# A routed two-layer network on one core: expert results are added into one row per token by indirect DMA, instead of being stored per choice and summed after a gather

## The reference

```
topv, topi = top_k(logits, K)            # K = 4, then 2
w   = softmax(topv)
sel = exp_out[token, topi]               # K rows of 128 per token
out = sum_k w[k] * sel[k]
x   = layernorm(x + out)
```

## Time and profile before

| | |
|---|---|
| median of 3 runs | 964.85 us (964.06 to 967.42) |
| span of the profiled execution, its own time | 1145.5 us |
| mean granted TensorE clock in it | 0.858 |
| PE / DVE / POOL / ACT busy | 73% / 57% / 46% / 45% |
| tiles of the first and second mixture | 76 and 36 (152 and 72 scatters of results) |

### The profile page before, as it was taken

The page is one execution under the profiler, slowest core; times in us unless marked ns, Lnnn a source line. Parts: engine busy times, 40 slices in busy tenths (PEclk is TensorE's granted clock), DMA queues, the critical chain, the costliest instruction groups (busy, mean ns, idle before and its releaser), DMA issues.

```text
span 1145.5 us, 35350 instructions
## 1 busy us (share of the span) xinstructions
PE 835.4 (73%) x11802; PEld 642.2 (56%) x11816; DVE 652.7 (57%) x1923; ACT 509.8 (45%) x1290; POOL 525.7 (46%) x538
## 2 busy tenths in 40 slices
PE   4898886877886513887788888847788839999920
PEld 1565555555565401766677667735555529888810
DVE  5457555455544520666565566647787636656656
ACT  2555444444433311544444445426454226656623
POOL 1013634546343471455554555541666644554433
PEclk9899888898857755999898999979887869999965
DMA  6011211112111123433333333323231124222243
GB/s 192 21 31 38 66 34 50 43 44 61 36 48 33 38 74 90 83 68 82 71 79 69 78 86 86 81 85 130 88 122 39 38 84 67 57 55 50 51 131 108
DMA packets 136238, 79.73 MB, mean 70 GB/s; under 512 B 104402, under 2 KB 116857, under 8 KB 136144
## 3 DMA queue, kind: packets, MB, share of 16 engines
q1 hardware_dynamic: 122256, 51.76, 18.7%
q0 software_dynamic: 13312, 25.31, 7.1%
q10 hardware_dynamic: 576, 1.34, 0.4%
HBM read 33.12 MB, written 32.63 MB: 57 GB/s over the span
## 4 chain that ended last, share of the span: by engine, by line
PE 48%; issue 13%; DVE 13%; another core or an unknown queue 9%; ACT 5%; SPq 4%; POOL 4%; DMA 2%; ACTq 1%; DVEq 0%; POOLq 0%
PE avbank L1736 6%; PE proj L1736 5%; PE avbank L1589 4%; PE t L1576 3%; PE t L1717 3%; PE s L1717 3%; PE s L1715 2%; PE t L1715 2%; PE s L1716 2%; PE t L1716 2%; ACT act_out L1359 2%; PE s L1539 2%; POOL xs L655 2%; PE t L1784 2%
## 5 line engine op out<-in xcount | busy, mean ns | idle before, releaser
L714 POOL DMA_INDIRECT yt<-ysb,to_now x224 | 236.8, 1057 | 260.7 <-ACT ysb L1346 197.4
L655 POOL DMA_INDIRECT xs<-x1p,sidx x192 | 189.8, 989 | 196.5 <-ACT prob L1265 111.7
L944 DVE CAST h_hi<-act_out 128x512 bf16<-128x512 f32 x152 | 73.6, 484 | 147.2 <-ACT act_out L1359 113.9
L945 DVE TENSOR_TENSOR h_lo<-act_out,h_hi 128x512 bf16<-128x512 f32 x152 | 107.9, 710 | 5.2
L1265 ACT ACTIVATE prob<-t 128x384 f32<-128x384 f32 (+1 forms) x160 | 74.4, 508 | 78.0 <-PE t L1576 66.1
L1715 PE MATMUL s<-xt,w_hi 128*128 128x256 bf16 x296 | 82.8, 280 | 17.8 <-DMA xt<-xs 13.3
L1736 PE MATMUL avbank<-w_hi,h_hi 128*128 x448 | 89.8, 230 | 7.6 <-issue 6.4
L1736 PE MATMUL avbank<-w_hi,h_lo 128*128 x448 | 87.7, 229 | 3.6 <-issue 3.3
L1736 PE MATMUL avbank<-w_lo,h_hi 128*128 x448 | 87.3, 228 | 2.4 <-issue 2.4
L1736 PE MATMUL proj<-w_hi,h_hi 128*128 x448 | 83.6, 220 | 7.2 <-DVE h_lo L945 5.6
L1717 PE MATMUL t<-xt,w_lo 128*128 128x256 bf16 x296 | 81.5, 275 | 5.9 <-issue 5.9
(11 more groups left out here) (235 smaller groups left out, 2131.4 us busy)
## 6 DMA issues: line engine op xcount, KB each, us to landing
w_raw<-w_all SPq DMA_DIRECT2D x59, 256.0 KB
gat<-yt SPq DMA_DIRECT2D x7, 1024.0 KB, 5.3
gat<-yt SPq DMA_DIRECT2D x10, 512.0 KB, 4.5
yt<-ysb,to_now POOLq DMA_INDIRECT x224
xs<-tail_rows SPq DMA_DIRECT2D x24, 129.0 KB
xs<-x1p,sidx POOLq DMA_INDIRECT x192
out<-ow SPq DMA_DIRECT2D x8, 256.0 KB, 2.3
xt<-xs SPq DMA_TRANSPOSE x112
```

The costliest lines, as they stand in the source:

```text
L655: pool.indirect_dma_start(out=xs[n][:, :], out_offset=bass.IndirectOffsetOnAxis(sidx[:, par, at:at + 1], 0), in_=x1p[:, par, t, k, :], in_ ...
L714: pool.indirect_dma_start(out=yt[n][:, :], out_offset=bass.IndirectOffsetOnAxis(to_now[:, u, s:s + 1], 0), in_=ysb[:, u, s, :], in_offset= ...
L944: ch.link(dve.tensor_copy(h_hi[:, par, c, :], act_out[:, par, c, :]))
L945: dve.tensor_tensor(h_lo[:, par, c, :], act_out[:, par, c, :], h_hi[:, par, c, :], ALU.subtract).then_inc(split_done[n], 1)
```

## The change

`yt` is gone. For each mixture there is `acc`, one row of 128 floats per token (and 256 rows for padding). It is filled with the residual (`fill_sums`, one 256 KB store per batch on SP, as soon as the batch's rows are kept). The weight of a choice travels with the row: two more bf16 places in `xs` hold it as a float, written by `weigh`. ACT multiplies by it when it takes a tile out of PSUM, with two activations of 128x128 in place of one copy of 128x256, and therefore waits for `to_loaded` now. The scatters add to `acc` instead of overwriting (`compute_op=ALU.add`), with no bounds check.

A tile's scatters wait until those of the preceding tile have landed; the two tiles may hold the same token for different choices. `scale_results`, `pair_up`, `add_up` and the weighted sums of `final_sums` are gone; a batch's load is 256 KB in place of 1024 KB or 512 KB, with 2 KB contiguous per partition (`acc[0]` and the output are laid out "(p t)"). The final scales are double buffered. `tile_table` gets one more column (`new_of`), which nothing reads; one more DVE operation, one more PE transpose and one more DVE conversion make it.

```
-                        pool.wait_ge(to_loaded[n][u], 16 * g + 16)
                         pool.wait_ge(y_done[n], RING * g + u + 1)
-                        pool.sem_inc(sending[n], 1)
+                        if u > 0 or not (type(g) is int and g == 0):
+                            pool.wait_ge(y_stored[n][u - 1 if u else RING - 1], 16 * S2 * (g + 1 if u else g))
+                        pool.sem_inc(sending, 1)
                         for s in range(S2):
                             pool.indirect_dma_start(
-                                out=yt[n][:, :], out_offset=bass.IndirectOffsetOnAxis(to_now[:, u, s:s + 1], 0),
-                                in_=ysb[:, u, s, :], in_offset=None, bounds_check=B * L * top[n] - 1,
-                                oob_is_err=False).then_inc(y_stored[n][u], 16)
+                                out=acc[n][:, :], out_offset=bass.IndirectOffsetOnAxis(to_now[:, u, s, 0:1], 0),
+                                in_=ysb[:, u, s, :], in_offset=None, compute_op=ALU.add).then_inc(y_stored[n][u], 16)
 
                 pool.wait_ge(table_kept[n], 1)
-                more = over_tiles(pool, n, group)
+                pool.wait_ge(acc_filled[n], 16 * B)
...
+            def fill_sums(n, b):
+
+                rows = acc[n][bass.ds(b * L, L), :]
+                rows = rows.rearrange("(p t) d -> p t d", p=P) if n == 0 else rows.rearrange("(t p) d -> p t d", p=P)
+                sp.wait_ge(x1_kept, B * n + b + 1)
+                apart(sp)
+                sp.dma_start(rows, xres[:, bass.ds(b * T, T), :]).then_inc(acc_filled[n], 16)
...
-                    act.wait_ge(yp_ready[n], j + 1)
                     if not (type(use) is int and use == 0):
                         act.wait_ge(y_stored[n][u], 16 * S2 * use)
-                    nc.scalar.copy(ysb[:, u, :, :], y_bank[u % 2][:, 0:S2 * D].rearrange("p (s d) -> p s d", s=S2)
-                                   ).then_inc(y_done[n], 1)
+                    act.wait_ge(to_loaded[n][u], 16 * use + 16)
+                    act.wait_ge(yp_ready[n], j + 1)
+                    for s in range(S2):
+                        ins = nc.scalar.activation(ysb[:, u, s, :], y_bank[u % 2][:, s * D:(s + 1) * D], ACT.Identity,
+                                                   scale=to_now[:, u, s, 1:2].bitcast(F32))
+                    ins.then_inc(y_done[n], 1)
...
                 if nxt:
-                    x2_apply(b + 1)
-                if nxt2:
-                    pair_up(b + 2, par)
-                    add_up(b + 2, par)
+                    x2_apply(b + 1, 1 - par)
                 take_logits(1, b)
...
                 if nxt2:
-                    y_stats()
+                    sum_stats(b + 2, par, i + 1)
```

More of the change, by code:

```diff
@@ L476, in _ @@
                     sp.dma_start(w_raw[:, k, :], w_all[:, bass.ds((2 * c + k) * CH, CH)]).then_inc(raw_in[k], 16)
+            def fill_sums(n, b):
[4 more added lines that the diff above has]
+                sp.dma_start(rows, xres[:, bass.ds(b * T, T), :]).then_inc(acc_filled[n], 16)
+            for c in range(1, CPB_0):
+                load_chunks(c)
+            with sp.Fori(2, B) as b:
+                for c in range(CPB_0 // 2):
+                    load_chunks(CPB_0 // 2 * b + c)
+                fill_sums(0, b - 2)
+            for b in range(B - 2, B):
+                fill_sums(0, b)
             def fill_tails(n):
@@ L554, in _ @@
             sp.wait_ge(all_stored[0], 1)
-            for half in range(2):
-                ts = slice(T // 2 * half, T // 2 * half + T // 2)
-                rows = slice(ts.start * P * K0, ts.stop * P * K0)
-                sp.dma_start(gat0[:, 0, ts, :, :], yt[0][rows, :].rearrange("(t p k) d -> p t k d", p=P, k=K0)
-                             ).then_inc(gathered[1][half], 16)
-            load_outputs(0, 1)
+            for b in range(2):
+                load_outputs(0, b)
             for b in range(B):
                 if b + 2 < B:
-                    sp.wait_ge(comb_done, b + 1)
+                    sp.wait_ge(x2_ready, b + 1)
                     load_outputs(0, b + 2)
+                if b:
+                    fill_sums(1, b - 1)
                 sp.wait_ge(lo_done, CHUNKS_0 + max(b - 1, 0))
@@ L1199, in _ @@
             dve.wait_ge(decay_ready, 1)
-            dve.wait_ge(x1_kept, B)
-            for half in range(2):
-                dve.wait_ge(gathered[1][half], 16)
-                for k in range(K0):
-                    for t in range(T // 2 * half, T // 2 * half + T // 2):
-                        ins = dve.scalar_tensor_tensor(out=y[:, t, :], in0=gat0[:, 0, t, k, :], scalar=wres[:, t, k:k + 1],
-                                                       in1=y[:, t, :] if k else xres[:, t, :], op0=ALU.mult, op1=ALU.add)
-                    if k < K0 - 1:
-                        ch.link(ins)
-            ins.then_inc(comb_done, 1)
-            dve.wait_ge(comb_done, 1)
-            y_stats()
-            x2_apply(0)
-            pair_up(1, 1)
-            add_up(1, 1)
-            y_stats()
+            sum_stats(0, 0, 0)
+            x2_apply(0, 0)
+            sum_stats(1, 1, 0)
             for e in range(T):
@@ L1702, in tile_table @@
                 pe.wait_ge(table_ready[n], 1)
[L1703 removed]
+                for c in range(3):
                     pe.transpose(xbank[0:1, c * P:(c + 1) * P], tile_e[:, 4 + c:5 + c], ident)
[L1706 removed]
+                ins = pe.matmul(xbank[0:1, 3 * P:3 * P + 1], tile_e[:, 3:4], fours[:, :], start=True, stop=True)
                 ins.then_inc(table_turned[n], 1)
```

178 lines of the change are left out of this document (76 added, 102 removed).

## The result

| | us |
|---|---|
| changed kernel, median of 4 runs | 1243.66 (1236.76 to 1246.38) |
| kernel before, beside it, median of 4 runs | 966.13 (964.06 to 967.76) |
| ratio | 1.2885, 95% interval 1.2833 to 1.2937 |
| predicted | 1045 (955 to 1150) |

The changed kernel is 29% slower. The direction was forecast, the size was not: the loss is 278 us where 80 were expected, and the time is outside the range.

The account below looks back on a forecast made before the run. It took PE and idle time to set the tiles now, and a serial scatter chain of 4.8 us per tile afterwards. Mixtures +60 and +19, savings and table -23: +56 on 1145.5, or 1012; with 1077 otherwise, the middle 1045 (955 to 1150).

Parts of the forecast that it names:

- The second way to the median: Both mixtures: tiles of 3.4 and 4.0 us grow to 4.8, adding 135 us, less 23 of savings: 1077 us.
- the recording stretches: Whole kernel: profiling lengthens the execution, so the 1145.5 us span stands for a median of 964.85, 0.842 of it.
- The middle between 1012 and 1077: Whole kernel: 1045 us, taken between shrinking everything alike (1012) and a chain that does not shrink (1077).
- a tile in series costs 1.28 + 2.41 = 3.69 us: Both mixtures: second scatter 1.28 us after the first, landing 2.41 us later, with plain scatters; 3.85 us mid-stage.
- an add does not repeat the issue on POOL: Result scatters of both mixtures: adding costs somewhat under half a round trip, 0.95 us per tile, larger descriptors included.
- The savings: Outside the tiles: stage (c)'s first load -5, six batches -4, final stage -15, larger table +1; 23 us saved.
- Cost 0 for ScalarE's take-out and its wait: Mixture tiles: two activations for one copy, +0.45 us per tile, hidden behind the chain; wait for `to_loaded` covered; cost 0.
- Rival 1: Mixtures: the wait is hidden, serial tile 3.7 to 3.85 us, only savings remain, about 942 us; chance 0.14.
- Rival 2: First mixture: PE's clock falls too, its tile lasts 5.5 us and PE is the bound, 1130 us; chance 0.10.
- Rival 3: Both mixtures: the add costs a whole trip, 6.26 us per tile, +276, 1240 us; chance 0.07.

Follow-up runs that it names:

- after_overwrite: Changed kernel with its scatters overwriting instead of adding, the wait for the preceding tile kept: 1094.15 us, ratio 1.1352.
- scatters_alone: No part of the kernel: 24 serial pairs of plain, then of adding scatters on an idle core, then again beside copies; alone 4.28 and 5.32 us per pair.
- before_serial: Kernel before with the new wait alone, each tile's plain scatters waiting for the preceding tile's to land: 1117.85 us, ratio 1.1589.
- weights_left_out: Changed kernel with ScalarE's old unweighted copy as take-out, not waiting for the tile's numbers (POOL waits for them): 1243.47 us beside 1243.66.
- hybrid_plain: Kernel before, own row per choice, no added waits; weight travels with the row, ScalarE applies it, final sums are wide additions: 969.32 us, ratio 1.006.

## Why the prediction was wrong

The chain was named rightly, and so was who waits for it; three terms were wrong, the tile before and the two parts of the tile in series. The second way to the median, by which a tile's growth is 1.4 and 0.8 us and the result 1077, makes the account. The growth was 5.99 - 2.92 = 3.07 us and 5.95 - 4.02 = 1.93. So 76 x 1.67 + 36 x 1.13 = 168 us are missing from it, and 1077 + 168 = 1245, which is the result to 1 us. The forecast of 1045 lacks 32 us more.

| per tile, us | forecast | measured, first / second mixture |
|---|---|---|
| tile before | 3.4 / 4.0 | 2.92 / 4.02 |
| plain tile in series | 3.85 | 4.70 / 4.54 (`after_overwrite`) |
| adding | 0.95 | 1.29 / 1.42 |
| tile after | 4.8 | 5.99 / 5.95 |

- **Step "the recording stretches" failed.** The second profile refutes it. It hid that the first mixture stood at 2.92 us per tile, with PE's own 2.76 and POOL's 2 x (1.07 + 0.30) = 2.73 just below. Half of the waiting of the earlier trace rows belonged to that one long execution: in the usual one 99.6 us of POOL's idle time end with `ysb`, not 197.4. This is 0.5 us per tile, 36 us. The middle between 1012 and 1077 went wrong for the same reason, by 32 us: there was nothing to shrink.
- **Step "a tile in series costs 1.28 + 2.41 = 3.69 us" failed.** The 2.41 us of the earlier trace rows end with a memset on POOL and a load on SP. A waiting plain scatter's record starts later: 3.00 us after the second one's start, with nothing else running (`scatters_alone`). The pair costs 4.28 us alone; in the kernel it costs 0.3 to 0.4 more, of which the weight load is 0.19 in the first mixture, and the prediction had allowed 0.16, read from the scatters' time on POOL, for all of that. This is 0.85 and 0.69 us per tile, 89 us.
- **Step "an add does not repeat the issue on POOL" failed.** It lengthens it, from 0.98 to 1.55 us, with 144 packets for 32. The 0.95 us had POOL's part in them without a row for it; POOL alone takes 0.58. Alone the price is 1.04 us, not far from 0.95; in the kernel it is 1.29 and 1.42, and there an adding pair's follower starts 4.1 us after its second scatter, against 3.45 alone (plain: 3.3 against 3.00). 0.34 and 0.47 us per tile are 43 us. That the extra packets make landings more sensitive to traffic is argued from the DMA engines' share (26% of the time in the adding pairs alone, 9% in the plain ones), not shown. The last two steps could also be divided otherwise: by the adding scatter that starts 2.50 us after a plain one, the restart was short by 0.09 us only, and adding costs 0.58 + 0.95 us; 3.69 + 0.09 + 1.53 is again the 5.3 us of the pair alone. In that division the landing's price was guessed rightly, and POOL's issue was the part left out.
- **The savings held.** Forecast -23, measured -23.7 (`after_overwrite` against `before_serial`). In the changed kernel itself they are 18 at the end, where 15 were forecast, and 3 in the linear attention, where 9 were. There the last landing takes 3.87 us in place of 2.41, and the granted clock was 0.79, against 0.80 before and 0.82 in `after_overwrite`, which gains 8 us in that stage; how much of the rest the clock explains was not tested.
- **Cost 0 for ScalarE's take-out and its wait held** in the changed kernel (`weights_left_out`), where the chain covers it. In `hybrid_plain`, without that cover, a tile of the first mixture took 0.06 us more.
- **Rival 1** was excluded by the wait alone, +154 us. **Rival 2**: the clock did fall, to 0.84 in the first mixture and 0.92 in the second, with PE busy for 65% and 69%. But PE's 294.5 us in 451.7 are 3.9 us of a tile of 6, so the chain is the longer of the two, as the forecast had it. **Rival 3** gave 1240 us and so the right time, by luck: it had 6.26 us per tile as 3.85 plus a whole trip of 2.41, over a tile before of 3.4. The true 5.97 are 4.65 plus 1.33, over 2.92. Its chance of 0.07 was small for a term that no row bore on.
- One reading was off without effect: the DMA engines' share in the stages shown was 27 to 33%, not 29 to 33%.

The Trainium skill (DMA: Bandwidth & Descriptors, Anatomy of one DMA — SWDGE (gpsimd) path) puts most of a transfer's fixed cost of 2 us into the receipt of the write. POOL's idle time before each plain pair, 2.03 us, is of that size, but it holds the restart too, and no run here separates the receipt from it. The 0.2 us of HBM's access latency on the same page (Latency and other measured facts), by which the prediction's estimate for the serial tile was 4.05 us, don't give the price of adding: the pairs alone cost 1.04 us more, and the measurement decides.

## What to carry to other kernels

A wait that puts transfers in series costs per transfer what issue, landing and restart are together, and it must be read between instructions of the kind that will follow: here 4.28 us for a plain pair, 3.69 by the memset that followed. Adding in the transfer saves work at the reader and takes it from the queue's issuer; before the engine that issues is counted as idle, see in a second profile that it is, and if the profiled time does not match the runs, take that profile again before any sum is made. If sums must be built this way, two tables taken in turn hide the landing (1017 against 1244 us, with the second table neither filled nor read), but here only rows of their own for each choice, with the cheaper end, beat the start, by 0.4%.

## What the runs showed of the hardware

- An indirect scatter of 128 rows of 512 B takes 0.97 us on POOL, and 1.55 with an add; 32 packets and 144. On an idle core a waiting plain scatter starts 3.00 us after the start of the plain one that it waits for; adding after adding takes 3.45, adding after plain 2.50.
- A serial plain pair took 4.28 us on an idle core, 4.5 to 4.7 in the kernel and 4.8 to 5.7 beside 200 GB/s of weight loads. An adding one took 5.32 on an idle core and 5.95 to 5.99 in the kernel.
- POOL's power of 128x4 took 1.56 us beside a wide VectorE addition and 1.04 without one. The Trainium skill (SBUF — State Buffer, Terms) says that these two engines share a pair of ports which one of them holds for a whole instruction. The 0.5 us agree with a wait of that kind; no run here separates it from another cause.
- One profiled execution of the kernel before spanned 1145.5 us, where a second one spanned 963.6 and none of the timed ones took over 969, with the first mixture's tile at 4.01 us, the attention at 461 us in place of 372 and its granted clock at 0.80 in place of 0.89.
